# Mixture-of-experts layer inside a perceiver block: the last 32 slots in one group of 192 small tiles, and another order of the weight pieces

## What is computed

```
xf = layernorm(x).reshape(1024, 512)
logits = xf @ Wg + bg                              # 8 experts
one_hot = one_hot(argmax(logits), 8)
h = gelu(einsum('td,edh->eth', xf, W1))            # W1: 8 x 512 x 2048
y = einsum('eth,ehd->etd', h, W2)                  # W2: 8 x 2048 x 512
out = x + einsum('etd,te->td', y, one_hot)
```

## Time and profile before

| | |
|---|---|
| median of 3 runs | 804.28 us |
| the profiled execution | 809.27 us, span 807.3 us, mean granted TensorE clock 0.983 |
| TensorE busy | 775.0 us (96%) |
| VectorE busy | 624.6 us (77%) |
| ScalarE busy | 471.0 us (58%) |
| GpSimd busy | 242.6 us (30%) |

### The profile page before, as it was taken

The page is one execution under the profiler, slowest core; times in us unless marked ns, Lnnn a source line. Parts: engine busy times, 40 slices in busy tenths (PEclk is TensorE's granted clock), DMA queues, the critical chain, the costliest instruction groups (busy, mean ns, idle before and its releaser), DMA issues.

```text
span 807.3 us, 22183 instructions
## 1 busy us (share of the span) xinstructions
PE 775.0 (96%) x8851; PEld 460.1 (57%) x8851; DVE 624.6 (77%) x990; ACT 471.0 (58%) x847; POOL 242.6 (30%) x413
## 2 busy tenths in 40 slices
PE   8989999999999999999999999995999999999995
PEld 3445545555445555455557544554967866876783
DVE  4977888879788888787768668788778788778860
ACT  4546666656665565665547133238568758857960
POOL 0235234433354433344430200012153241331220
PEclk9999999999999999999999999996999999999998
DMA  8324453344413345323523511104899988998500
GB/s 306 140 64 109 106 155 94 80 107 108 94 41 93 94 107 134 64 71 106 122 55 57 209 53 53 53 0 137 287 386 415 405 348 290 350 350 301 230 31 15
DMA packets 94901, 125.56 MB, mean 156 GB/s; under 512 B 76352, under 2 KB 79168, under 8 KB 83956
## 3 DMA queue, kind: packets, MB, share of 16 engines
q1 hardware_dynamic: 92260, 117.65, 45.6%
q0 software_dynamic: 2576, 7.02, 2.4%
HBM read 100.47 MB, written 6.88 MB: 133 GB/s over the span
## 4 chain that ended last, share of the span: by engine, by line
PE 81%; DVE 11%; ACT 3%; DMA 2%; issue 1%; POOL 1%; SPq 1%; POOLq 0%; DVEq 0%; ACTq 0%
PE bank L1474 60%; PE bank L1852 10%; PE bank L1643 4%; DVE arena L933 3%; PE bank L1824 3%; PE bank L1609 3%; ACT arena L695 2%; DVE arena L989 1%; DMA arena<-arena 1%; DMA arena<-in_wv_t 1%; DVE arena L995 1%; ACT arena L662 1%; PE bank L1811 1%; DVE arena L948 1%; DVE arena L965 1%
## 5 line engine op out<-in xcount | busy, mean ns | idle before, releaser
L1474 PE MATMUL bank<-arena 128*128 128x160 f16 (+8 forms) x3944 | 562.9, 303 | 8.2 <-DVE arena L1366 2.0
L1474 PEld LDWEIGHTS bank<-arena 128*128 128x128 f16 (+2 forms) x3944 | 322.4, 100 | 236.6 <-issue 13.8
L662 ACT ACTIVATE arena<-arena 128x256 f16<-128x256 f32 (+5 forms) x302 | 254.1, 889 | 21.8 <-PE bank L1824 7.9
L933 DVE SCALAR_TENSOR_TENSOR arena<-arena 128x2048 f16<-128x2048 f32 (+4 forms) x102 | 200.5, 1987 | 37.5 <-ACT arena L662 34.6
L662 ACT ACTIVATE arena<-bank 128x512 f16<-128x512 f32 x175 | 100.1, 584 | 144.4 <-PE bank L1474 110.6
L933 DVE SCALAR_TENSOR_TENSOR arena<-bank,arena 128x512 f16<-128x512 f32 x174 | 116.8, 682 | 44.4 <-ACT arena L662 40.8
L1852 PE MATMUL bank<-arena 128*128 128x512 f16 x384 | 86.6, 379 | 0.0
L695 ACT ACTIVATE arena<-arena 128x257 f32<-128x257 f32 x128 | 63.5, 498 | 21.9 <-DVE arena L997 21.9
L528 POOL TENSOR_TENSOR arena<-arena 32x1024 f16<-32x1024 f32 (+1 forms) x16 | 34.1, 2132 | 140.1 <-PE bank L1643 139.9
L1852 PEld LDWEIGHTS bank<-arena 128*128 128x128 f16 x384 | 36.1, 98 | 41.1
L545 POOL COPY arena<-arena 32x256 f16 (+1 forms) x128 | 50.3, 393 | 24.0 <-DVE arena L933 11.8
(11 more groups left out here) (112 smaller groups left out, 486.1 us busy)
## 6 DMA issues: line engine op xcount, KB each, us to landing
arena<-in_w SPq DMA_DIRECT2D x64, 1024.0 KB, 6.8
arena<-in_ctx_t SPq DMA_DIRECT2D x15, 1024.0 KB, 5.4
arena<-in_awt SPq DMA_DIRECT2D x3, 1024.0 KB, 7.1
l_dram<-arena SPq DMA_DIRECT2D x4, 512.0 KB, 4.4
x_dram<-arena SPq DMA_DIRECT2D x1, 2048.0 KB, 13.7
arena<-in_wk_t SPq DMA_DIRECT2D x4, 256.0 KB, 4.8
arena<-in_ctx_t SPq DMA_DIRECT2D x4, 256.0 KB, 6.8
arena<-in_wv_t SPq DMA_DIRECT2D x1, 1024.0 KB, 8.2
```

The source lines that it names most:

```text
L662: return a.activation(dst, src, ACT.Copy, scale=scale)
L933: return v.scalar_tensor_tensor(dst, src, scale, h, ALU.mult, ALU.subtract)
L1474: last = m.matmul(out_ap, w, x, start=(n == 0), stop=(n == len(pairs) - 1))
```

## The change

last_slots is called once per expert, after c = 3, with all four parts: 192 small tiles in one group. y_ps goes up once per expert. Pieces 4 and 5 of the next expert can't be split during this one any more, since TensorE reads those buffers to its end, so the order of the pieces changes: 4, 5, 6, 7 of this expert at k = 0, 2, 4, 6 and 0 to 3 of the next behind the loop, on ScalarE and on VectorE. Expert 0's pieces 4 and 5 are still split ahead of it, and its 6 and 7 at k = 4 and 6.

```diff
@@ ScalarE, after the second activation of each k
-                    if k == 0:
-                        if prev:
-                            act.wait_ge(s["y_ps"], n * 2)
-                        piece_hi(n, PIECES - 2)
-                    elif k == 2:
-                        piece_hi(n, PIECES - 1)
-                    elif nxt and k % 2 and k > 1:
-                        piece_hi(n + 1, k // 2 - 1)
+                    if k % 2 == 0:
+                        if prev and k == 0:
+                            act.wait_ge(s["y_ps"], n)
+                        if prev or k > 2:
+                            piece_hi(n, 4 + k // 2)
                 if nxt:
-                    piece_hi(n + 1, 3)
-                    act.wait_ge(s["y_ps"], n * 2 + 1)
-                    piece_hi(n + 1, 4)
-                    piece_hi(n + 1, 5)
+                    for k in range(4):
+                        piece_hi(n + 1, k)
@@ VectorE, rows_out
-                dve.wait_ge(s["y_ps"], n * 2 + 2)
+                dve.wait_ge(s["y_ps"], n + 1)
@@ VectorE, after the low half of each k
-                    if k == 0:
-                        piece_lo(n, PIECES - 2)
-                    elif k == 2:
-                        piece_lo(n, PIECES - 1)
-                    elif nxt and k == 3:
-                        piece_lo(n + 1, 0)
+                    if k % 2 == 0 and (prev or k > 2):
+                        piece_lo(n, 4 + k // 2)
                 if nxt:
-                    for k in range(1, 4):
+                    for k in range(4):
                         piece_lo(n + 1, k)
-                if nxt:
                     gathered(n + 1)
-                    for k in range(4, PIECES - 2):
-                        piece_lo(n + 1, k)
@@ TensorE, second layer
-                    if c % 2:
-                        last_slots((c - 1, c))
+                    if c == KC - 1:
+                        last_slots(range(KC))
```

More of the change, by code:

```diff
@@ L884, in _ @@
             gate_transpose_out(HT + 3)
-            for k in range(4, PIECES - 2):
-                piece_hi(0, k)
+            piece_hi(0, 4)
+            piece_hi(0, 5)
             def expert(n, prev=True, nxt=True):
@@ L919, in _ @@
                 with act.Fori(1, ROUNDS) as r:
-                    act.wait_ge(s["y_ps"], r * (2 * E))
+                    act.wait_ge(s["y_ps"], r * E)
                     for k in range(PIECES - 2):
```

## The result

The changed kernel takes 825.80 us (median of four runs, 825.08 to 826.76), the kernel before 804.53 in the four runs beside it: a ratio of 1.0267 [1.0253, 1.0281] (in brackets the 95% interval, here and below), 21.3 us slower. The forecast was slower by 2.9 us, and the time lies far outside the range of 800.5 to 810.0. The profiled execution took 826.76 us, span 825.0.

A forecast was written before the change was run, and what follows sets the result against it. TensorE bounds before; after, the ScalarE and VectorE chain to the token copies. Experts 1 to 6 at 27.46 + 1.5 us gave +3.5, expert 0 gave 0, the end -0.6: +2.9, so 807.2 us, range 800.5 to 810.0.

The forecast's parts named there:

- The holes in the first group go too: TensorE's idle hole in the first group of small tiles, 0.64 us in expert 2, was to vanish.
- the hole should not come back: Beside the gather, 36 wide matmuls now run; a queue of 64 instructions covers late supply for 6.9 us of them.
- Rival E: TensorE's 192 tiles outrun their instructions, moving the hole to each expert's end: 0.65 us more, 801.6 us; chance 0.04.
- A: Token copies bound experts 1 to 6, third GELU 1.0 to 1.84 us late: 804.2 to 809.2 us; chance 0.47.
- For the clock I count nothing: No clock cost for TensorE's idle stretches of 1.5 us, as it is busy for 26 us on either side.
- TensorE's own period, 27.38: One small-tile group less saves TensorE 0.22 us per expert, making its period 27.38 us.
- The chain, 27.41 + 0.05: ScalarE and VectorE splits end the token copies 27.41 us into an expert; 0.05 until TensorE follows makes 27.46.
- Lateness of 1.5 us: ScalarE's third GELU starts 1.5 us late in each of experts 1 to 6, put down to GpSimd's scatter; bounds 0 and 1.81.
- The ends: Expert 1's start unchanged, 0 (bounds -0.2 and +1.3); the kernel's end, with its second scatter, 0.6 us earlier.
- rival D: At the first boundary, piece 3 of expert 1 lands late, adding 1.3 us: 806.0 to 808.5 us; chance 0.07.
- The range: Whole kernel between 800.5 and 810.0 us, said to omit B's lower part and A's upper end.
- B: GELU lateness goes, as the scatter finishes before the third GELU's input is due: 798.2 to 800.6 us; chance 0.22.

The follow-up runs named there:

- order_only: Changed kernel with two groups of 96 small tiles again, so only the order of the pieces differs from before; 803.80 us, 1.0002 times the kernel before.
- four_groups: Changed kernel with four groups of 48 small tiles, one after each c; 812.25 us against 809.32 for the kernel before, 1.0035.
- order_loop: Changed kernel with two groups of 96 small tiles and TensorE's experts 1 to 6 as a hardware loop; 811.81 us, 1.0034 times the kernel before.
- after_light: Changed kernel with only an eighth of the bytes of each weight piece of experts 2 to 7 loaded; 815.17 us, 1.0073 times the kernel before.
- after_pad: Changed kernel with 64 more small matmuls on TensorE ahead of the experts; 831.57 us in one run, the kernel before 803.56.
- copies_first: Changed kernel with VectorE's token copies ahead of the four low halves of the next expert's pieces; 824.18 us, 1.0251 times the kernel before.
- after_loop: Changed kernel with TensorE's experts 1 to 6 as a hardware loop instead of written out; 810.30 us, 1.0085 times the kernel before.

## Why the prediction was wrong, step by step

**"The holes in the first group go too", "the hole should not come back".** This step failed, and it makes the miss: the forecast ran TensorE through the 192 tiles without a stop, and the runs showed breaks in the supply of its instructions, 18.1 us in experts 1 to 6, with 6.4 us of lowered clock behind them. The forecast judged cover by what lies beside the gather (36 wide matmuls) and by a queue of 64 instructions. It took GpSimd's gather for the cause of the 0.40 us hole in the earlier trace rows. That cause isn't shown either: order_only has the gather beside the same group (619.21 to 622.28 in expert 1, 3.1 us, where it lasted 4.5 beside the hole) and no hole in it. Nor do those holes look like the blocks. Before, they stand after 74, 58, 61 and 72 tiles in experts 1, 2, 4 and 5, without the steady step of 12; here expert 1:

```profile
623.18 0.52 PE L1824 MATMUL bank<-arena 128*32 128x128 f16 x22 [0.41 <-issue]
```

Their cause stays open. For the large breaks, what had to be asked is how long a block of 256 instructions lasts. Wide matmuls make it last 128 x 0.216 = 28 us, first-layer ones 8.9 (128 x 13.29 / 192), and 128 small tiles 128 x 14 ns = 1.8. Two groups of 96 never fill a block; the shortest one in order_only, 88 tiles and 40 matmuls of the next first layer, lasts 4.0 us and made no break there, but one of 76 tiles and 52 matmuls, 4.7 us, made one of 0.32 us, and of 1.16 in the two later runs. In the changed kernel the mixture of 88 and 40 did break, for 1.7 us. The Trainium skill, page "TensorE: Matmul & The Clock Gate" (Engine queue depths in Part 1), gives TensorE a queue of 64 instructions. An estimate from that depth is 32 pairs, which bridge 0.45 us of small tiles; breaks of 4 us stand within them here.

**Rival E, the burst that outruns its instructions.** It was the right one, at a chance of 0.04. It was priced at 0.65 us per expert, the size of the hole in a group of 96 tiles, "which hides under A". Measured: 3.9 to 4.2 us in every second expert, 1.7 to 2.3 more in the first layers of the same experts, and 1.6 of clock. It was weighed down because no second group and no group of expert 6 has a hole. But no group of 96 can hold a whole block, and the small holes of before, used for and against it, are another thing (above), so those rows could say nothing of it. The Trainium skill, page "Runtime: NRT & Kernel Launch" (Instruction fetch mechanics), has blocks of 256 instructions, and the distances in this trace agree. It also has the refill mostly hidden, since dispatch is slower. That agrees with blocks of wide or first-layer matmuls alone, which show no break here, and not with the ones that do break, which hold 76 small tiles or more.

**"For the clock I count nothing."** Wrong: 1.6 us each, four times. The forecast had idle stretches of 1.5 us in mind. Behind breaks of 1.5 and 1.8 us (experts 3 and 1) the clock did stay up; behind 2.05 and the large ones it fell.

**TensorE's own period, 27.38.** Right: 27.39 from its parts, against 27.61 with two groups. One group less does save 0.22 us.

**The chain, 27.41 + 0.05.** Right to 0.01 us in order_only. In the changed kernel the copies end 28.91 to 28.94 after the start in experts 2, 4 and 6, against the forecast's 28.91, and TensorE is not made to wait, since the slow first layer delays it by the same 1.5 us from which the chain starts.

**Lateness of 1.5 us.** Right in size (third GELU at 6.91, 6.95 and 6.92 in experts 2, 4 and 6, 5.42 undisturbed), wrong in cause. Here it is the clock and the breaks in the first layer, not GpSimd's scatter. In order_only the scatter starts 1.31 us after each expert's start, earlier than ever before, and nothing is late; so the argument from the earlier trace rows falls. It did rest on an execution that lay 5 us above the median. On the chip with 809.3 us the forecast's lateness and wait are there (four_groups, order_loop), at a total loss near the forecast's; how much of it is the chain's, and what makes the GELU late, stays open.

**The ends.** Expert 1 began 1.5 us earlier, not 0: expert 0 itself started 1.3 earlier, and piece 3 was not late (rival D has nothing for it). The last stretch is 1.2 us longer than order_only's where -0.6 was forecast, by its break of 1.2.

**The range.** 800.5 to 810.0 is said to leave out the lower part of B and the upper end of A. It leaves out nearly all of B (798.2 to 800.6, chance 0.22) and nothing of A (up to 809.2). Neither edge had a term for breaks of the measured size.

## What to carry to other kernels

Before merging short instructions into a long run, divide it into blocks of 256 instructions and ask how long the shortest one lasts: here 1.8 us cost breaks of 4 us, and 4 us cost nothing in one order of transfers and 1.7 in another. Idle time named "issue" that moves by a constant step from one repetition to the next is a sign of supply; without the step, as in the small holes of the kernel before, it is no such sign. A few instructions inserted far ahead (breaks move) or a hardware loop (breaks go) settle it. A profiled execution 5 us above its median is poor ground for a mechanism that depends on its lateness: on two chips order_only had none of it.

## What the runs showed of the hardware

- Beside about 400 GB/s of weights a block of TensorE instructions took nearly 6 us (1.8 us of tiles and a break of 4; changed kernel, expert 1). With an eighth of the bytes (after_light), or none (expert 7 of the changed kernel), it took some 3 us, and in after_pad's expert 6, with none, there was no break.
- A break of 2.05 to 4.13 us was followed by a granted clock of 0.50 to 0.68 for the next 4 us in all cases but one, in the one-group kernels and order_loop. That one followed a break of 3.58:

```profile
692.70:696.70 4.00, 4.00 (x80) 3.90 (x80) 0.82 (x2) 1.53 (x3) 1.57 (x2) 1.00 0.84 344
```

  It is in copies_first, at the start of expert 4. Why it kept its clock is open.
- A loop on TensorE cut the instruction packets from 18 to 2 over five experts. Where it jumps back, TensorE began 0.17 us (order_loop) to 0.24 us (after_loop) later behind its copies than where it doesn't.
- The kernel before took 803.6, 803.8 and 809.3 us on three chips. On the last one ScalarE's third GELU is late by some 1.3 us in the experts of the changed order. The changed kernel took 825.8 and 829.9 us in two sets of runs.
